# Moving the packing of two binary samples from VectorE to GpSimd in the second pass of a two-layer block

## The reference

```python
x = x + _L0_conv_ref(_gn(x), ...)      # an 8x8 algebra product over groups of 64 values, and a bias
x = x + _L1_conv_ref(_gn(x), ...)
# inside the second, with h the group-normalised x and res the same:
h = sign(batchnorm(h))
h = conv3x3(h, sign(conv_w) * scale, groups=16)    # 512 channels, padding 1
h = batchnorm(h) + res
h = where(h > 0, h, a * h)
```

## Time and profile before

| | us |
|---|---|
| median of 3 runs | 4704.78 (4703.31 to 4704.99) |
| the profiled execution, its time | 4701.64 |
| its span | 4699.4 |
| busy: TensorE, VectorE, ScalarE, GpSimd | 4509.8, 4235.9, 3861.5, 1478.8 |
| granted TensorE clock, mean | 0.992 |

### The profile page before, as it was taken

One profiled execution on the slowest core, in us unless ns is written; L12 is line 12 of the kernel. 1 busy time (PEld: TensorE's weight loads), 2 busy tenths in 40 slices (PEclk: granted clock), 3 DMA queues, 4 the chain that ended last, 5 costly groups with the idle time before them and its releaser, 6 DMA issues.

```text
span 4699.4 us, 83432 instructions
## 1 busy us (share of the span) xinstructions
PE 4509.8 (96%) x21948; PEld 2748.6 (58%) x22204; DVE 4235.9 (90%) x10523; ACT 3861.5 (82%) x5517; POOL 1478.8 (31%) x3481
## 2 busy tenths in 40 slices
PE   6999999999999979999999996999999999999999
PEld 6999999999999974433333332444444444444444
DVE  6999999999999989999999997888888888888887
ACT  7999999999999967777777774777777777777776
POOL 4888888888888880000000000000000000000000
PEclk9999999999999999999999998999999999999999
DMA  5888888888888879999999996999999999999998
GB/s 202 318 317 316 318 319 318 317 318 320 321 317 317 317 282 351 370 369 368 368 368 368 369 368 252 377 375 376 374 376 375 376 377 374 377 375 375 376 376 297
DMA packets 686229, 1612.17 MB, mean 343 GB/s; under 512 B 30002, under 2 KB 423986, under 8 KB 620658
## 3 DMA queue, kind: packets, MB, share of 16 engines
q1 hardware_dynamic: 686194, 1611.76, 95.0%
HBM read 940.55 MB, written 671.10 MB: 343 GB/s over the span
## 4 chain that ended last, share of the span: by engine, by line
PE 76%; POOL 6%; ACT 6%; issue 5%; DVE 5%; DMA 1%; SPq 0%; DVEq 0%; POOLq 0%; ACTq 0%
PE psV L1007 13%; PE psT L1066 12%; PE psV L1066 12%; PE psT L1082 8%; PE psT L1084 7%; PE psV L1084 7%; PE psV L1082 7%; PE psT L990 7%; DVE ring_x L952 4%; ACT ring_y L675 3%; PE psV L1004 3%; POOL ring_y L481 2%; ACT ring_g L584 1%; POOL u_r L495 1%; POOL x_r L457 1%
## 5 line engine op out<-in xcount | busy, mean ns | idle before, releaser
L1007 PE MATMUL psV<-W0T,ring_gT 128*128 128x128 f32 x8192 | 1080.0, 275 | 47.6 <-issue 34.0
L1007 PEld LDWEIGHTS psV<-W0T,ring_gT 128*128 128x128 f32 x8192 | 1076.8, 192 | 33.6
L770 DVE BATCH_NORM_STATS2 early<-ring_z 128x6 f32<-128x128 f32 x4096 | 822.7, 274 | 0.0
L761 DVE SCALAR_TENSOR_TENSOR ring_z<-psV,x_r,ring_x 128x1024 f32<-128x1024 f32 x512 | 657.2, 1284 | 117.3 <-DVE early L770 76.9
L665 ACT ACTIVATE late<-ring_x,minus_b 128x512 f32<-128x512 f32 x1024 | 639.5, 707 | 1.3 <-PE psV L1084 1.3
L632 ACT ACTIVATE ring_x<-ring_x,bn_c 128x1024 f16<-128x1024 f32 x512 | 604.2, 1229 | 31.0 <-DMA bn_c<-bn_scratch 31.0
L850 DVE BATCH_NORM_STATS2 h_tup<-ring_x 128x6 f32<-128x512 int16 x1024 | 619.4, 668 | 0.0
L481 POOL TENSOR_SCALAR ring_y<-ring_z,u_r,u_nm 128x1024 f32<-128x1024 f32 x512 | 605.8, 1199 | 35.6 <-POOL gn L500 35.6
L964 DVE SCALAR_TENSOR_TENSOR ring_x<-ring_x,bn_q,psV 128x512 f32<-128x512 f32 x512 | 376.1, 744 | 255.2 <-PE psV L1084 254.9
L590 ACT ACTIVATE ring_g<-ring_x,x_ms 128x1024 f32<-128x1024 f32 x512 | 585.3, 1143 | 0.0
L675 ACT ACTIVATE ring_y<-ring_y,gnb 128x512 f32<-128x512 f32 x512 | 368.0, 801 | 239.7 <-DVE ring_x L952 202.3
(11 more groups left out here) (150 smaller groups left out, 5857.6 us busy)
## 6 DMA issues: line engine op xcount, KB each, us to landing
ring_x<-in_x SPq DMA_DIRECT2D x128, 2048.0 KB, 8.8
y_scratch<-ring_y SPq DMA_DIRECT2D x128, 2048.0 KB, 12.7
ring_x<-y_scratch SPq DMA_DIRECT2D x512, 512.0 KB, 6.2
out<-ring_x SPq DMA_DIRECT2D x256, 1024.0 KB, 14.0
h_scratch<-ring_x SPq DMA_DIRECT2D x256, 512.0 KB, 6.1
ring_y<-y_scratch SPq DMA_DIRECT2D x128, 1024.0 KB, 7.3
ring_z<-y_scratch SPq DMA_DIRECT2D x128, 1024.0 KB, 7.4
ring_g<-h_scratch SPq DMA_DIRECT2D x64, 1024.0 KB, 11.6
```

Of the source, the lines that this page charges most:

```text
L761: dve.scalar_tensor_tensor(out=ring_z[:, c % 2, cols], in0=psV[:, j % 2, :], scalar=x_r[:, s, j:j + 1], in1=ring_x[:, s, cols], op0=ALU.mu ...
L770: last = dve.bn_stats(z_tup[:, s, j, 2 * r:2 * r + 2, :].rearrange("p h t -> p (h t)"), ring_z[:, c % 2, SL * j + 2 * S * r:SL * j + 2 * S ...
L1007: last = pe.matmul(psV[:, j % 2, P * r:P * (r + 1)], ring_gT[:, j, P * r:P * (r + 1)], W0T[:, :], start=False, stop=(r % 4 == 3))
```

## The change

GpSimd takes over the packing. It needs two instructions for it: it multiplies the high half by 1024 in place in the sign slot, as soon as that half's sign is taken, and then adds the low half into the frame. ScalarE takes the high half first. GpSimd's packing stands in its program behind the 16 instructions of L553 and ahead of the `pow` of the second batch norm. VectorE loses its pack, and its `flip` moves behind two waits on its own semaphores.

```diff
@@ gpsimd, behind L554
             last.then_inc(diag_done, 1)
+
+            def pack(i, c):
+                t = SLOTS * i + c
+                low, high = (sign_slot(c % 2)[:, e] for e in range(2))
+                pool.wait_ge(signed, 2 * t + 1)
+                pool.sem_inc(pack_begun)
+                pool.tensor_scalar(high, high, PACK, None, ALU.mult).then_inc(raised, 1)
+                pool.wait_ge(signed, 2 * t + 2)
+                pool.wait_ge(raised, t + 1)
+                if from_round(i, c, 2):
+                    pool.wait_ge(conv_done, t - 1)
+                frame = padded[:, c % 2, :].rearrange("p (r b) -> p r b", b=PAD)
+                low, high = (part.rearrange("p (r b) -> p r b", b=SIDE) for part in (low, high))
+                pool.tensor_tensor(frame[:, IMG:IMG + SIDE * IMG, 1:1 + SIDE], high, low, ALU.add).then_inc(packed, 1)
+
+            rounds(pool, pack, T2, 2 * HEAD)
+
             pool.wait_ge(bn2_step, BN2_VE)
@@ scalar, take_sign
-                for e in range(2):
+                for e in (1, 0):
@@ vector
-            def pack(i, c):
-                t = SLOTS * i + c
-                dve.wait_ge(signed, 2 * t + 2)
-                if from_round(i, c, 2):
-                    dve.wait_ge(conv_done, t - 1)
-                frame = padded[:, c % 2, :].rearrange("p (r b) -> p r b", b=PAD)
-                low, high = (sign_slot(c % 2)[:, e].rearrange("p (r b) -> p r b", b=SIDE) for e in range(2))
-                dve.scalar_tensor_tensor(out=frame[:, IMG:IMG + SIDE * IMG, 1:1 + SIDE], in0=high, scalar=PACK, in1=low,
-                                         op0=ALU.mult, op1=ALU.add).then_inc(packed, 1)
@@ vector, pass2
-                if from_round(i, c, 3):
-                    flip(i, c - 3)
                 if from_round(i, c, 8) and c % J == 0:
                     dve.wait_ge(h_kept, i + c // J - 1)
                 if from_round(i, c, 4):
                     dve.wait_ge(h_counted, SLOTS * i + c - 3)
-                pack(i, c)
+                if from_round(i, c, 3):
+                    flip(i, c - 3)
```

More of the change, by code:

```diff
@@ L252, in two_layer_kernel @@
         signed = sem("signed")
+        pack_begun = sem("pack_begun")
+        raised = sem("raised")
         packed = sem("packed")
```

## The result

The changed kernel takes 4911.02 us (median of 4 runs, 4910.22 to 4911.98), the kernel before 4704.05 beside it (4703.17 to 4704.99). The ratio is 1.044, with a 95% interval of 1.0426 to 1.0457. The forecast was 4849, the range 4694 to 5080.

A forecast was written before the change was run, and what follows sets the result against it. It took VectorE to bound pass 2 before and GpSimd after: 1.83 + 2.21 + 0.09 + 0.68 = 4.81 us a step, 256 steps from 1766.7 us, +144 us, so 4849 us; range 4694 to 5080.

The forecast's parts named there:

- The sign: Whole kernel: the change makes it slower, +3.1% against the median; slower by over 0.2% had chance 0.77.
- the bound: Pass 2 after the change: GpSimd becomes the bound at 4.81 us a step, above TensorE's 4.205.
- the multiplication: GpSimd, each step of pass 2: times 1024 over 1024 values takes 1.83 us, bounds 1.20 and 3.23.
- the flip: VectorE's flip in pass 2: it and GpSimd's instructions exclude each other, adding 0.68 us to GpSimd's step.
- the second rival: Pass 2: GpSimd's work fits under TensorE's 4.205 us a step; -9.6 us, 4695; chance 0.18.
- 1.5 to 2.73 us: Multiplication lengths on GpSimd counted as the forecast's own case (4764 to 5079); chance 0.45.
- VectorE bound the kernel before: Pass 2 from 1944 us on: VectorE bounds at 4.273 us a step, TensorE behind it at 4.205.
- 14.6 us: Pass 2: the most that freeing VectorE can bring, 214 steps x 0.068 us, 0.3% of the kernel.
- the end of the pass: End of pass 2 (unpack, flip, statistics of the last steps): claimed the same in both kernels.
- The sum, 2.21 us: GpSimd, each step of pass 2: adding the low half into the frame, 2.21 us, bounds 1.7 and 2.54.
- The gaps, 0.09 us a step: GpSimd in pass 2: the sum starts 0.09 us after the multiplication it waits for ends.
- The start, GpSimd free at 1766.7: Start of pass 2: packs wait behind L553's 16 instructions, 9.3 us without VectorE's packs, until 1766.7 us.

The follow-up runs named there:

- e1: The changed kernel with GpSimd's multiplication written with two operations (times 1024, plus 0.0) in place of one; 4688.76 us.
- e4: The changed kernel with the multiplication moved to VectorE, the sum alone on GpSimd and the diagonals (L553's 16 instructions) behind the packs; 4684.8 us.
- e6: The changed kernel with a two-operation multiplication on GpSimd, and the 16 diagonal instructions behind the packs, also with two operations; 4684.18 us.
- e9: The changed kernel with GpSimd's multiplication written as two multiplications (times 1024, times 1.0); 4688.48 us.
- run 36: Not a follow-up run: "run" is a verb here, and the 36 matmuls are two steps of TensorE, which take 8.41 us at its own pace.
- e3: The changed kernel with the 16 instructions of the diagonal matrices behind GpSimd's packs in place of ahead of them; 4907.2 us.
- e10: The changed kernel with its one-operation multiplication written to unused memory in place of back over its input; 4910.43 us.
- e2: The changed kernel with a flip over 4 words in place of 1024, so output is not the reference's; 4910.13 us.
- e8: The changed kernel with the two-operation multiplication and a second sum into unused memory ahead of the sum; 5104.18 us.
- e7: The changed kernel with its one-operation multiplication split into two instructions of 512 values; 5014.91 us.
- e5: The kernel before, with VectorE's pack in two instructions (multiplication, then sum) in place of one; 4721.7 us.

## Why the prediction was right, and where it was not

The sign, the bound and the range held; the time was 62 us short, the remainder of two larger errors of opposite sign. That it came so near, and within the range, is luck. With the multiplication alone put right the forecast would have been 5090, outside the range; with the flip alone put right GpSimd's step would have been 4.13 us, and the forecast that of the second rival, 4695. The multiplication also lies outside the 1.5 to 2.73 us that went with the forecast. Against the span of before, 210.2 us more, the steps come out as follows.

- **VectorE bound the kernel before, by 0.068 us a step, with TensorE at 4.205 close behind:** right. e1, e4, e6 and e9 all run 36 matmuls in 8.41 us. That 14.6 us is the most that it can bring was not: e4 and e6 gained 18.1 and 18.7 us, since the end of the pass became shorter too (last point).
- **The multiplication, 1.83 us:** too low by 0.94, or 241 us over the pass. This is the term that failed most. The rows had it: L553's 593 ns for 128 values with L492 gave 2.94 ns a value, and 2.5 were measured; L492 has one operation as L553 has. I put 170 ns of L553 down to reading its factor and took the loop from a two-input instruction. e3 and e6 show that the excess over the two-operation form is 225 ns with the factor read from memory in both, so the whole of those 170 belongs to the one-operation form, as e1, e9 and e10 show for fp16.
- **The sum, 2.21 us:** 2.12 measured, 23 us less. The frame's rows of 8 cost nothing.
- **The gaps, 0.09 us a step:** there are two, and with the first steps they come to 5.08 - 2.77 - 2.12 = 0.19 us, 25 us more.
- **The flip, 0.68 us of GpSimd's step:** wrong. It was 174 us of the forecast, and e2 puts it at nothing. That the two exclude each other was right (the flip grew to 1.03, 0.51 us even when shortened), but not that it is held for the whole of every instruction. The slow multiplication lets VectorE in after 0.90 us of its 2.77, and in the steady steps the flip always comes in that instruction. Where it holds, in e8, the price is 0.40. The section of the "SBUF — State Buffer" page of the Trainium skill that I weighed (Who interferes with whom) has the exclusion last for the whole instruction: the sum agrees with it to within 0.13 us, since the first flip took 2.67 us beside a sum of 2.14; the one-operation multiplication doesn't.

```profile
1781.50 2.14 POOL L570 TENSOR_TENSOR late<-ring_x 128x1024 f16<-128x1024 f16 x1
...
1781.52 2.67 DVE L853 TENSOR_SCALAR ring_x<-ring_x 128x1024 int32<-128x1024 int32 x1 [21.78 <-ACT ring_x L662]
```

- **The start, GpSimd free at 1766.7:** right, 1768.33 less the 1.6 us of pass 1. e3, which takes the diagonals out of the way, is 3.8 us faster.
- **The sum of it:** 144 + 241 - 23 + 25 - 174 = 213, and 1.6 from pass 1. The end of the pass, which I had as equal, gave 5.9 back. Before, 31.9 us lay between the last matmul (2858.4) and the first affine of pass 3 (2890.3); after, 26.0 (3073.5 to 3099.5). Pass 3 took 1.0 us more. That makes 210. e1 shows the gain at the end too: its last matmul comes 9.1 us earlier than before's, as the forecast's second rival had it, and its pass 3 starts 13.3 us earlier. In it the last store of the pass left SyncE 2.8 us after the last flip, against 7.3 us before. These are the rows of the chain that ended last, of e1; rows 12 show the flip they answer to:

```profile
2850.36 0.70 DVE ring_x L853
...
2851.06 2.79 SPq L384
...
2853.90 16.35 DMA h_scratch<-ring_x
```

Why SyncE issues that store sooner was not tried and stays open.

The second rival was the true course of e1: everything under TensorE's 4.205 us. The rule that I set beside it, from the page "GPSIMD Engine Reference" of the Trainium skill (4.1, Engine selection), that one-input operations run at about line rate, holds for the two-operation form here (1.05 us for 1024 values) and not for the one-operation form (2.77 us).

## What to carry to other kernels

Before work goes to an engine that has been idle, find a row of the same instruction form there, not of a similar one: the count of operations in one GpSimd instruction changed its price by 2.6 times, and with it the result from 4% slower to 0.3% faster. A second operation that does nothing (plus 0.0) is worth a trial on GpSimd. And ask first how far behind the second limit stands: here it was 1.6% of a step, so that even a free move could bring 0.3 to 0.4% of the kernel.

## What the runs showed of the hardware

- GpSimd's TENSOR_SCALAR over 1024 fp16 values takes 2.77 us with one operation and 1.05 us with two, whether the second is an addition or a multiplication, and whether or not it works in place (e1, e9, e10). In f32 over 128 values, with the factor from memory, it is 602 and 377 ns (medians of e3 and e6). In both types the one-operation form costs 1.7 to 1.8 ns a value more. Multiplication is the only single operation that was tried.
- GpSimd keeps out VectorE's flip, an instruction between two SBUF tiles, for 0.90 us from the start of a one-operation multiplication of 1024 values, 0.48 us for 512, 0.91 us for the two-operation one of 1024 and 2.0 us for the sum of two inputs of 1024. Only in the one-operation form is this much less than the instruction's length; there the flip makes the 2.77 us no longer, and the 1.49 us of 512 values 0.13 longer (changed kernel, e7, e1, e8).
- VectorE's TENSOR_SCALAR over 1024 fp16 values takes 0.43 us, its sum of two fp16 inputs 0.89, and both in one instruction 1.22; two instructions took longer than one (e4, e5).
